# Two places for a waiting buffer, and another order inside an attention slot: a macaron block on one NeuronCore

## The reference, cut to what matters

```python
x = x + 0.5 * ffn(layernorm(x), W_fc, W_proj)
x = x + attn(layernorm(x), Wq, Wk, Wv, bv, Wo, bo)
x = x + 0.5 * ffn(layernorm(x), W_fc, W_proj)

def ffn(x, W_fc, W_proj):           # 256 -> 1024 -> 256
    y = square(relu(x @ W_fc.T)) @ W_proj.T
    return spikes(y) / 5             # 5 steps of a leaky integrator, a count of spikes
def attn(x):                         # 16 heads of 16
    q, k = rope(x @ Wq.T), rope(x @ Wk.T)
    v = x @ Wv.T + bv
    p = softmax(where(causal, q @ k.T / 4, -inf))
    return (p @ v) @ Wo.T + bo
```

## Time and profile before

| what | value |
|---|---|
| median of 3 runs | 1331.09 us (1330.83 to 1335.95) |
| the profiled execution | 1329.68 us |
| its span, first to last instruction | 1328.0 us |
| TensorE, matmuls | 1250.2 us busy (94%), 8224 |
| VectorE | 1098.4 us busy (83%) |
| ScalarE | 886.5 us busy (67%) |
| GpSimd | 256.0 us busy (19%) |
| mean granted TensorE clock | 0.975 |
| chain that ended last | PE 73%, DVE 16%, ACT 5%, issue 3% |

### The profile page before, as it was taken

The page is one execution under the profiler, slowest core; times in us unless marked ns, Lnnn a source line. Parts: engine busy times, 40 slices in busy tenths (PEclk is TensorE's granted clock), DMA queues, the critical chain, the costliest instruction groups (busy, mean ns, idle before and its releaser), DMA issues.

```text
span 1328.0 us, 22227 instructions
## 1 busy us (share of the span) xinstructions
PE 1250.2 (94%) x8224; PEld 761.0 (57%) x8224; DVE 1098.4 (83%) x2592; ACT 886.5 (67%) x1229; POOL 256.0 (19%) x205
## 2 busy tenths in 40 slices
PE   5999999967899999999999999999999989999996
PEld 5888888944444444434444444444344336988996
DVE  4567777787699999999999999999999844777876
ACT  6766666521277777777777777777777777566654
POOL 5003333442210210120210201101101122222300
PEclk9999999978799999999999999999999989999998
DMA  3124444973481350530710901703501140344311
GB/s 134 41 72 151 151 152 135 176 224 103 100 117 32 53 87 11 84 55 11 117 23 10 138 10 27 113 10 49 90 11 48 44 119 27 106 133 134 97 33 64
DMA packets 87701, 109.26 MB, mean 82 GB/s; under 512 B 25292, under 2 KB 59852, under 8 KB 85964
## 3 DMA queue, kind: packets, MB, share of 16 engines
q1 hardware_dynamic: 87592, 107.83, 34.9%
HBM read 64.09 MB, written 41.68 MB: 80 GB/s over the span
## 4 chain that ended last, share of the span: by engine, by line
PE 73%; DVE 16%; ACT 5%; issue 3%; SPq 2%; DMA 1%; DVEq 0%; POOL 0%; ACTq 0%
PE m_ps L1196 21%; PE o_ps L1234 19%; PE s_ps L1218 7%; DVE maxes L1131 6%; PE yps_c L697 5%; PE ups_a L678 5%; PE ups_c L678 5%; PE yps_a L697 4%; DVE masked L1134 4%; PE gps_a L744 3%; PE gps_c L729 2%; PE gps_a L729 2%; ACT probs L1109 1%; DMA kT<-qkT_parts 1%; PE tps_a L722 1%
## 5 line engine op out<-in xcount | busy, mean ns | idle before, releaser
L1109 ACT ACTIVATE probs<-s_ps 128x1024 f32<-128x1024 f32 (+3 forms) x640 | 538.7, 896 | 191.6 <-PE s_ps L1218 190.6
L1131 DVE TENSOR_REDUCE maxes<-m_ps 128x1 f32<-128x512 f32 x768 | 495.1, 684 | 45.3 <-PE m_ps L1196 33.8
L1196 PE MATMUL m_ps<-kT,qT 64*128 64x512 f32 (+3 forms) x1280 | 415.0, 431 | 28.3 <-DVE maxes L1134 10.1
L1196 PEld LDWEIGHTS m_ps<-kT,qT 64*128 64x128 f32 x1280 | 194.1, 186 | 351.0 <-DVE maxes L1131 194.3
L1218 PE MATMUL s_ps<-qT,kT 64*128 64x512 f32 (+3 forms) x1280 | 307.3, 395 | 7.1 <-ACT probs L1109 6.9
L1234 PE MATMUL o_ps<-probs,v_w 128*32 128x512 f32 (+3 forms) x2560 | 302.4, 545 | 0.2 <-POOL probs L1078 0.2
L1134 DVE CUSTOM_DVE_ANT_0 masked<-m_ps,mask 128x128 f32<-128x128 f32 (+3 forms) x512 | 227.8, 482 | 10.2 <-PE m_ps L1196 8.6
L1078 POOL TENSOR_SCALAR_AFFINE_SELECT probs<-probs 128x512 f32<-128x512 f32 x128 | 82.4, 644 | 640.1 <-ACT probs L1109 640.1
L1218 PEld LDWEIGHTS s_ps<-qT,kT 64*128 64x128 f32 x1280 | 163.5, 187 | 36.9 <-ACT probs L1109 32.9
L572 DVE TENSOR_TENSOR h_lo_a<-hsq_a,h_hi_a 128x512 fp32r<-128x512 f32 x64 | 52.0, 812 | 61.5 <-ACT hsq_a L375 40.0
L1234 PEld LDWEIGHTS o_ps<-probs,v_w 128*32 128x32 f32 x2560 | 50.6, 108 | 72.6 <-issue 59.8
(11 more groups left out here) (136 smaller groups left out, 1899.1 us busy)
## 6 DMA issues: line engine op xcount, KB each, us to landing
qT<-qkT_parts SPq DMA_DIRECT2D x96, 128.0 KB
kT<-qkT_parts SPq DMA_DIRECT2D x48, 256.0 KB
qkT_parts<-qk_hi_a SPq DMA_DIRECT2D x32, 256.0 KB, 4.5
qkT_parts<-qk_lo_a SPq DMA_DIRECT2D x32, 256.0 KB, 4.7
sumsT<-osum SPq DMA_DIRECT2D x32, 256.0 KB, 2.6
table_a<-in_rot SPq DMA_DIRECT2D x8, 768.0 KB, 7.0
xin_a<-in_x SPq DMA_DIRECT2D x8, 512.0 KB, 3.6
xres_a<-in_x SPq DMA_DIRECT2D x8, 512.0 KB, 4.7
```

What stands on the lines that cost most here:

```text
L1109: act.activation(probs[:, b % PBUF, 2 * hp:2 * hp + 2, off:CH], s_ps[hp][:, :, off:CH], ACT.Exp, scale=D ** -0.5).then_inc(exp_done, 1)
L1131: last = dve.tensor_reduce(out, m_ps[:, i % MB, 0:width], AX.X, ALU.max)
L1196: last = pe.matmul(m_ps[:, i % MB, at:at + width], qT[n % 2][r0:r0 + HR, j, hp, t * P:(t + 1) * P], kT[n % 2][r0:r0 + HR, hp, k * CH:k * C ...
```

## The change

It has three parts.

1. **A second pair of banks in the tail.** `pair_bank` lets `project_pair(c, 1)` of the last three chunks write into `tps`. It then no longer waits for `turn_pair(c, 0)`, and `project_v` waits only for that one. The projections move one slot ahead (f = 2 to 1 and 4 to 3), and `turn_pair(c, 0)` of the last two chunks from f = 0 to f = 1. The transposes `turn(xm)` now wait for the turns that read `tps`.
2. **A fourth bank for the led items.** The 69 items ahead of slot 0 go round four banks, the three of `m_ps` and `o_ps`, which has no other use until slot 2. `BANK` names the bank of each item and `BANK_AHEAD` the item that had it last. The first item behind them (item 69) takes the bank of item 68. The very first products wait until the last led item in `o_ps` has been read.
3. **The order of a slot.** `products` and the second `scores` change places.

No instruction that computes is added or taken away.

```diff
+    def pair_bank(c, x):
+
+        return tps if x == 1 and c >= NC - 3 else gps
...
         def turn_pair(c, x):
+            bank = pair_bank(c, x)
...
-                dve.tensor_tensor(turned[:, m], gps[:, :, :], table[:, c % 2, m:m + 2, :], ALU.mult)\
+                dve.tensor_tensor(turned[:, m], bank[:, :, :], table[:, c % 2, m:m + 2, :], ALU.mult)\
                    .then_inc(s["turn_done"], 1)
...
-            if first and f in (0, 3) and has(it, 3):
-                turn_pair(it - 3, f // 3)
+            if first and f == (1 if it > NC else 0) and has(it, 3):
+                turn_pair(it - 3, 0)
+            if first and f == 3 and has(it, 3):
+                turn_pair(it - 3, 1)
...
-            else:
+            elif bank is gps:
                 wait(pe, "turn_done", 4 * c + 2)
...
-            wait(pe, "turn_done", 4 * c + 4)
+            wait(pe, "turn_done", 4 * c + (4 if pair_bank(c, 1) is gps else 2))
...
             if first and f == 5 and has(it, 2):
                 wait(pe, "mid_norm", it - 1)
+                if has(it, 3) and pair_bank(it - 3, 1) is tps:
+                    wait(pe, "turn_done", 4 * (it - 3) + 4)
                 turn(xm, "mid_T")
...
-            if first and f == 2 and has(it, 3):
+            if first and f == (2 if it < NC else 1) and has(it, 3):
                 project_pair(it - 3, 1)
-            if first and f == 4 and has(it, 3):
+            if first and f == (4 if it < NC else 3) and has(it, 3):
                 project_v(it - 3)
...
+LED = sum(g < 0 for g, _ in ORDER)
+BANK = [i % (MB + 1) if i < LED else (i - LED) % MB for i in range(len(ORDER))]
+BANK_AHEAD = [max([k for k in range(max(0, i - 2 * MB), i) if BANK[k] == BANK[i]], default=-1) for i in range(len(ORDER))]
+LAST_LED = max(i for i in range(LED) if BANK[i] == MB)
...
+    def bank(i):
+        return o_ps if BANK[i] == MB else m_ps[:, BANK[i], :]
...
-            wait(pe, max_read, ITEM[e] - MB + 1)
+            wait(pe, max_read, BANK_AHEAD[ITEM[e]] + 1)
...
+                if n == j == 0:
+
+                    pe.wait_ge(max_read, LAST_LED + 1)
...
             scores(n, j, b, 0)
             ring(items[q[1]:q[2]])
-            scores(n, j, b, 1)
-            ring(items[q[2]:q[3]])
             if g >= 2:
                 products(*SLOTS[g - 2])
+            ring(items[q[2]:q[3]])
+            scores(n, j, b, 1)
             ring(items[q[3]:])
```

More of the change, by code:

```diff
@@ L743, in project_pair @@
                                                  ((proj_hi, mT_hi), (proj_hi, mT_lo), (proj_lo, mT_hi))]):
-                    last = pe.matmul(gps[:, ab, :], wt[:, k, n0:n0 + P], x_[:, k, :],
+                    last = pe.matmul(bank[:, ab, :], wt[:, k, n0:n0 + P], x_[:, k, :],
                                      start=(i == 0), stop=(i == 3 * EC - 1))
@@ L1130, in unit @@
                 if k < j:
-                    last = dve.tensor_reduce(out, m_ps[:, i % MB, 0:width], AX.X, ALU.max)
+                    last = dve.tensor_reduce(out, bank(i)[:, 0:width], AX.X, ALU.max)
                 else:
-                    last = dve.tensor_tensor_reduce(masked[:, i % MB, at:at + width], m_ps[:, i % MB, at:at + width],
+                    last = dve.tensor_tensor_reduce(masked[:, BANK[i], at:at + width], bank(i)[:, at:at + width],
                                                     mask[:, CH - width:CH], 1.0, NEG, ALU.add, ALU.max, out)
@@ L1157, in shift_out @@
             wait(dve, shift_in, SHIFTS * step_no(e[1], e[2]))
-            dve.tensor_copy(shiftT[:, :], m_ps[0:2 * G * T, i % MB, 0:P]).then_inc(max_read, 1)
+            dve.tensor_copy(shiftT[:, :], bank(i)[0:2 * G * T, 0:P]).then_inc(max_read, 1)
         pending = []
@@ L1195, in unit @@
             for t, hp, k, width, at in parts:
-                last = pe.matmul(m_ps[:, i % MB, at:at + width], qT[n % 2][r0:r0 + HR, j, hp, t * P:(t + 1) * P],
+                last = pe.matmul(bank(i)[:, at:at + width], qT[n % 2][r0:r0 + HR, j, hp, t * P:(t + 1) * P],
                                  kT[n % 2][r0:r0 + HR, hp, k * CH:k * CH + width], start=True, stop=True)
@@ L1203, in turn_shift @@
             pe.wait_ge(neg_step, 3 * step_no(e[1], e[2]) + 3)
-            pe.transpose(m_ps[0:2 * G * T, i % MB, 0:P], negparts[:, :, :].rearrange("p a c -> p (a c)"), ident[:, :])\
+            pe.transpose(bank(i)[0:2 * G * T, 0:P], negparts[:, :, :].rearrange("p a c -> p (a c)"), ident[:, :])\
               .then_inc(max_done, 1)
@@ L1313, in build @@
     memory = Memory(nc, feed)
-    for n, shape in (("masked", [P, MB, CH]), ("maxes", [P, 2, 2, G // 2, T, NJ]), ("negmax", [P, G * T]), ("negparts", [P, 2, G * T]),
+    for n, shape in (("masked", [P, MB + 1, CH]), ("maxes", [P, 2, 2, G // 2, T, NJ]), ("negmax", [P, G * T]), ("negparts", [P, 2, G * T]),
                      ("shiftT", [2 * G * T, P])):
```

## The result

The changed kernel takes **1350.01 us** (median of 4 runs, 1344.49 to 2306.94; one run lies far off the other three, 1344.49, 1348.53 and 1351.50, and does not set the ratio; without it the median is 1348.53). The kernel before, on the same chips, takes 1333.32 us (4 runs, 1330.83 to 1335.95). The ratio is **1.0108**, 95% interval 1.0079 to 1.0138: slower by 1.1%, where 1321 us and a range of 1312 to 1330 had been forecast. The largest part of the loss has the mechanism of rival (c), which had a chance of 0.08; its time was 1340.

The account below looks back on a forecast made before the run. VectorE was taken to bound attention, with no engine the bound in the tail, where VectorE and TensorE take turns. The terms -10.6 + 1.5 + 0 - 0.7 = -9.8 took 1329.68 to 1319.9, with 1.41 for the median 1321 us; range 1312 to 1330.

Parts of the forecast that it names:

- rival (c): End of each j: o_ps copy ends later, TensorE stands, VectorE runs dry; up to 0.60 at 31 places, 1340 us; chance 0.08.
- The tail: Projections ahead of attention: VectorE's five long stops shrink from 16.7 to 6.1 us, -10.6 us.
- project_v(6): Tail: VectorE's stop at this projection shrinks from 4.95 to 2.0 us.
- pair 1 of chunk 7: Tail: VectorE's stop at this projection shrinks from 3.95 to 1.0 us.
- project_v(7): Tail: TensorE needs 5.6 us against 4.8 of cover, so VectorE's stop shrinks from 3.68 to 0.8.
- pair 0 of chunk 7: Tail: no turn beside it, but it starts earlier; VectorE's stop shrinks from 3.39 to 2.3 us.
- rival (a): Tail: TensorE's clock comes back to 2.4 GHz, giving 1316 us; chance 0.24 together with another rival of the same time.
- The hand-over: From led items to slot 0: item 69 takes item 68's bank, first scores have less queued; +1.5 us, 0 to +3.
- The order inside a slot: Attention's slots: the loop of 2.70 us stays, gains and losses balance; 0 us, from -6 to +7.
- one unit (0.6) earlier: First products of each j: 0.6 earlier against 0.44 of slack, a wait of 0.2; none where slack is 0.77.
- What gets better: Attention's slots: pairs of scores stand half a slot apart, and TensorE no longer meets ScalarE's second exponential; bound -6 us.
- The end: From 1060 us on: ScalarE's gap of 0.25 goes, last products come 0.5 later; -0.7 us, between -2 and +1.

Follow-up runs that it names:

- e1: The changed kernel with the old order in a slot, so only the tail's changes: 1321.93 us, ratio 0.9907 to the kernel before.
- e3: The changed kernel with the old order (second scores ahead of products) in the slots b = 2: 1329.00 us, ratio 0.9965 to the kernel before.
- e4: The changed kernel with ScalarE's copy of o_ps moved between the two exponentials of its slot: 1328.91 us, ratio 0.9963 to the kernel before.
- e7: e1 with the banks behind the led items moved on by one, so item 69 avoids item 68's bank: 1320.87 us, ratio 0.9908.
- e10: e7 with the old order in b = 0, 1, 2 of every j and the new one elsewhere: 1319.25 us, ratio 0.9893.
- e2: The kernel before with the new order in a slot alone: 1358.55 us, ratio 1.0186 to the kernel before.
- e9: e7 with the new order only in slots on the diagonal with b of 3 or more: 1318.38 us, ratio 0.9892.
- e11: e10 with the old order also in the slots that hold a transpose of the maxima: 1330.52 us, ratio 0.9978.

## Why the prediction was wrong, step by step

**The tail, -10.6 forecast.** Right in sum, within what one profile can tell: 355.22 to 344.79 for the first scores is -10.4 (e1 -9.6, e3 -12.9, e4 -8.0). That e1's 1321.93 meets the forecast's 1321 is in part luck: the forecast started from a median of 1331.09 over three runs, and the 19 runs beside e1 have 1333.5, so e1 gained 12.4, not 9.1. The terms of the tail were less good. For project_v(6) and pair 1 of chunk 7, 2.0 and 1.0 had been forecast, and no stop is left; project_v(7) kept 2.21 where 0.8 had been forecast; pair 0 of chunk 7 kept 2.39 (2.3). The errors cancel, 4.6 against 6.1, with a new 1.00 and 1.10 further ahead (at 287 and 280 us).

At project_v(7) both sides of the comparison were off. It starts at 328.61 and VectorE's next unit at 334.79: TensorE needs 6.2 us where 5.6 had been put. VectorE is at its turn at 330.25 already, so the cover is 1.6 us of banks and 2.33 of turns, 4.0 where four full banks and the turns, 4.8, had been put. 6.2 - 4.0 = 2.2. The cover of 4.0 comes again in e3, but there the need is 4.8 and the stop 0.80, and in e7 and e10 this projection leaves no stop. The list of instructions is the same up to there; what differs in the rows is the clock (the changed kernel, e3, e7; the 24 matmuls of project_v(7)):

```profile
328.60:334.10 5.50, 5.50 (x27) 5.27 (x26) 3.98 (x8) 1.01 (x1) 3.82 (x3) 0.50 0.14 32
```

```profile
327.60:331.90 4.30, 4.30 (x27) 4.17 (x26) 3.94 (x8) 0.96 (x1) 2.67 (x2) 0.69 0.01 4
```

```profile
331.10:334.20 3.10, 3.10 (x27) 2.97 (x26) 3.10 (x9) 0.50 (x1) 2.41 (x1) 1.00 0.02 5
```

So a single stop of the tail can't be forecast to better than some 2 us, whatever the rule for the cover.

**The clock, rival (a).** As a mean it did not come back: 0.75 before, 0.74 now over the same stretch, though VectorE's five long stops shrank by 12 us and all its idle in the stretch from 17.2 to 8.9. From 274.95 to 341.50 it was 0.74 in the kernel before, 0.72 in e2 with the same tail, and 0.71 to 0.77 in the eight kernels that have both changes of the tail. It is uneven inside the stretch:

```profile
319.00:325.00 6.00, 5.22 (x23) 3.48 (x23) 6.00 (x17) 0.00 (x0) 0.00 (x0) 1.00 0.01 3
...
330.00:336.00 6.00, 5.51 (x26) 4.63 (x24) 3.79 (x7) 1.82 (x2) 4.58 (x3) 0.62 0.44 137
```

Pair 1 of chunk 7 (321.68 to 324.70) ran at clock 1.00 and left no stop; in e7 it took 4.2 us and left 0.71. project_v(7) behind it ran at 0.50. The Trainium skill (TensorE: Matmul & The Clock Gate, A second HAM failure mode) describes a kernel that cycles through PSUM banks and whose clock goes back and forth between the two levels. The trace agrees that the clock goes back and forth in the tail. That fewer waits keep it up is what the prediction drew from this; over the whole tail the trace does not bear that out.

**The hand-over, +1.5.** Its two parts can be seen, the 0.88 ahead of the first scores, and 0.7 more from first scores to slot 40 (e1 97.3, before 96.6, from the same starts). But e7, which takes the cause away, is no faster than e1, so the price isn't confirmed.

**The order inside a slot, 0 (from -6 to +7): this is the step that failed.** It cost 25 us. The loop of 2.70 us stayed at the place of the earlier trace rows, as said. But the slack at the first products of each j was mis-sized on both sides. I let the products come "one unit (0.6) earlier" and left the copy where it was: 0.44 - 0.6, a wait of 0.2. In the trace the products are ready 0.42 earlier (3.27 in e4 against 3.69), and the copy ends 0.47 later (3.72 against 3.25), because ScalarE's second exponential now waits for its scores. Slack 0.44 - 0.42 - 0.47 = -0.45. The rows for it were there: the earlier trace rows is the end of a chain of two exponentials without a gap, and the change takes away just that. At the place of the earlier trace rows, with 0.77 of slack and no wait forecast, the products wait too, 0.20, and VectorE idles 0.49:

```profile
575.08 0.64 PE L1255 MATMUL o_ps<-probs,v_w 128*32 128x512 f32 x4 [0.20 <-ACT osum L1115]
```

```profile
576.61 0.69 DVE L1149 TENSOR_REDUCE maxes<-m_ps 128x1 f32<-128x512 f32 x1 [0.49 <-PE m_ps L1214]
```

And the place with the least slack, 0.26 at the end of each group, was not read at all; it waits longest, 0.57.

At 31 places 0.48 on average is 15 us of the 25; rival (c) had 0.60 and 18.6. It named the later copy, queue, victim and count rightly, and was given 0.08 because it was weighed against the slack of the trace before, with the copy where it had been. Another 0.8 a group, 6 us, is the rest of the new order: a cost in the first three slots of a j and a small one in full slots, less the gain on the diagonal (the table above); where it lies is shown, by which wait it comes is not. Some 4 us more lie in the first and the last group.

**"What gets better"** was half right: the new order does win 0.4 a group on the diagonal (e9 against 93.05), some 3 us, but in full slots it costs 0.2 net.

**The end, -0.7.** Wrong in sign and small. ScalarE's gap of 0.25 shrank to some 0.19, it did not go, and the last products end 0.6 later behind the first scores of the last slot (0.5 had been forecast). From the first scores of slot 310 to the last products it is 20.9 us where it was 20.5.

```profile
1107.91 3.77 ACT L1127 ACTIVATE probs<-s_ps 128x1024 f32<-128x1024 f32 x4 [0.19 <-PE s_ps L1236]
```

## What to carry to other kernels

When an instruction moves ahead of another in one engine's list, follow both through every engine that they feed: what moved back delays its consumer, and what is queued behind that consumer is late with it. Slack measured before the change is slack between two moving ends, and both must be moved before they are compared. An engine that waits a little for its input has room at that very place: the copy put into ScalarE's gap of 0.36 us took 1.9 us off each group without touching TensorE's order. Where such a place comes several times in a period, read the slack at each; here it was 0.26 to 0.77. And where an order helps in some slots only, it can be used in those alone, but look at the seams between the two orders: e11's cost 0.65 us of waiting at one place.

## What the runs showed of the hardware

- Over the tail the mean granted clock stayed at 0.74 to 0.75 while VectorE's five long stops fell from 16.7 to 4.6 us; within it, 12 matmuls of a pair took 3.0 us at clock 1.00 (321.68 to 324.70) in one place and a stretch 5 us later was back at 0.62.
- With the same list of instructions up to there, the 24 matmuls of project_v(7) took 5.5 us at clock 0.50 in the changed kernel, 4.3 at 0.69 in e3 and 3.1 at 1.00 in e7, and the first scores of attention started between 342.33 and 347.17 us (e3, e4).
- A stop of TensorE passed on whole: 0.42 us of waiting ahead of the products gave VectorE 0.67 us of idle at the same place, of which 0.22 is there in every full slot anyway. Nothing of it was absorbed there.
